# Two transformer layers on one core: the first two heads' score operands loaded ahead of the rest, and fewer unread products in front of them

## The reference, cut to what matters

```python
x = x + L0_attn(layernorm(x))      # rotary positions, 16 heads
x = x + L0_ffn(layernorm(x))       # one shared and 7 routed experts
x = x + L1_attn(layernorm(x))      # 16 heads
x = x + L1_ffn(layernorm(x))       # relative attention, then 32 experts
scores = q @ k.T / sqrt(8); out = softmax(scores) @ v
```

## Time and profile before

| what | value |
|---|---|
| median of three executions | 2069.04 us |
| the three | 2067.9, 2069.04, 2098.41 us |
| the profiled execution's own time | 2086.47 us |
| its span, first to last instruction | 2084.7 us |
| its mean granted clock of TensorE | 0.953 |
| PE busy / DVE busy / ACT busy | 94% / 66% / 58% of the span |

### The profile page before, as it was taken

The page is one execution under the profiler, slowest core; times in us unless marked ns, Lnnn a source line. Parts: engine busy times, 40 slices in busy tenths (PEclk is TensorE's granted clock), DMA queues, the critical chain, the costliest instruction groups (busy, mean ns, idle before and its releaser), DMA issues.

```text
span 2084.7 us, 40739 instructions
## 1 busy us (share of the span) xinstructions
PE 1966.8 (94%) x13972; PEld 1183.6 (57%) x13972; DVE 1379.4 (66%) x1770; ACT 1207.1 (58%) x2289; POOL 517.9 (25%) x501
## 2 busy tenths in 40 slices
PE   7999999799988999999769999999999999987998
PEld 4333334577764333333446666666666666665887
DVE  5999996656656689999554555545555455336776
ACT  2799999366641679999514444444444444443554
POOL 4000000278862000000032222222222222103654
PEclk9999999799997579999989999999999999988999
DMA  5333333131106123332341111221111122014654
GB/s 179 123 98 107 98 106 99 45 133 62 51 0 196 55 75 107 98 106 91 109 127 48 48 47 47 61 53 49 47 47 47 47 63 51 10 32 164 224 211 146
DMA packets 82559, 182.99 MB, mean 88 GB/s; under 512 B 16048, under 2 KB 45488, under 8 KB 77136
## 3 DMA queue, kind: packets, MB, share of 16 engines
q1 hardware_dynamic: 82448, 181.49, 28.0%
HBM read 146.83 MB, written 36.31 MB: 88 GB/s over the span
## 4 chain that ended last, share of the span: by engine, by line
PE 46%; DVE 2%; DMA 1%; SPq 1%; issue 0%; ACT 0%; DVEq 0%
PE PS L799 17%; PE PS L883 8%; PE PS L811 6%; PE PS L785 6%; PE PS L794 4%; PE PS L774 4%; DVE M L1278 1%; DMA Ks<-in_kv 0%; SPq L384 0%; PE PS L818 0%; PE PS L598 0%; PE PS L589 0%; PE PS L757 0%; DMA k_stack<-PR_r 0%; SPq L364 0%
## 5 line engine op out<-in xcount | busy, mean ns | idle before, releaser
L1257 DVE TENSOR_REDUCE M<-PS 128x1 f32<-128x1024 f32 x512 | 598.4, 1218 | 49.8 <-PE PS L676 44.9
L1540 ACT ACTIVATE PR<-PS 128x512 f32<-128x512 f32 x1024 | 540.1, 601 | 63.2 <-PE PS L691 42.7
L1577 ACT ACTIVATE PR<-PS 128x512 f32<-128x512 f32 x512 | 306.2, 599 | 376.9 <-PE PS L799 373.1
L1278 DVE TENSOR_REDUCE M<-PS 128x1 f32<-128x1024 f32 x256 | 311.9, 1222 | 219.3 <-PE PS L785 212.2
L701 PE MATMUL PS<-PR,Va 128*32 128x256 f32 x4096 | 343.6, 409 | 16.0 <-POOL Va L1724 7.7
L691 PE MATMUL PS<-Qs_r,Ks_r 25*128 25x512 f32 x1024 | 311.9, 520 | 0.0
L676 PE MATMUL PS<-Ks_r,Qs_r 24*128 24x512 f32 x1024 | 272.5, 527 | 1.7 <-DMA Ks_r<-k_stack 1.4
L676 PEld LDWEIGHTS PS<-Ks_r,Qs_r 24*128 24x128 f32 x1024 | 100.1, 192 | 217.8 <-issue 160.9
L1273 DVE TENSOR_TENSOR rt<-PS,rel 128x512 f32<-128x512 f32 x128 | 88.5, 691 | 159.4 <-PE PS L757 157.9
L701 PEld LDWEIGHTS PS<-PR,Va 128*32 128x32 f32 x4096 | 84.5, 110 | 154.3 <-issue 77.1
L1724 POOL TENSOR_TENSOR Va<-Vt,nil 128x64 f32<-128x64 f32 x96 | 28.0, 295 | 563.0 <-PE PS L701 559.5
(11 more groups left out here) (204 smaller groups left out, 3129.6 us busy)
## 6 DMA issues: line engine op xcount, KB each, us to landing
Qs<-g_dram SPq DMA_DIRECT2D x29, 1024.0 KB, 4.8
Ks_r<-k_stack SPq DMA_DIRECT2D x256, 100.0 KB
Qs_r<-q_stack SPq DMA_DIRECT2D x256, 96.0 KB
Qs_r<-q_stack SPq DMA_DIRECT2D x128, 128.0 KB
Ks_r<-k_stack SPq DMA_DIRECT2D x128, 128.0 KB
o_dram<-Ob SPq DMA_DIRECT2D x96, 128.0 KB, 2.7
Ks<-g_dram SPq DMA_DIRECT2D x10, 1024.0 KB, 4.9
q_stack<-BIG_r SPq DMA_DIRECT2D x18, 256.0 KB, 3.2
```

The source lines that it names most:

```text
L1257: e.tensor_reduce(M[:, s, qt:qt + 1], PS[:, 2 + 2 * (qt % 2):4 + 2 * (qt % 2), :] .rearrange("p a b -> p (a b)"), AX.X, ALU.max, negate=Tr ...
L1278: e.tensor_reduce(M[:, s, qt:qt + 1], PS[:, bk:bk + 2, :].rearrange("p a b -> p (a b)"), AX.X, ALU.max, negate=True).then_inc(max_done, 1)
L1540: e.activation(PR[:, kt % 4, qh * GW:(qh + 1) * GW], bank(RING[(x + turn) % 3]), ACT.Exp, scale=SCALE).then_inc(exp_done, 1)
L1577: e.activation(PR[:, kt % 4, qh * GW:(qh + 1) * GW], bank(TURN[kt % 2][qh]), ACT.Exp)\
```

## The change

It splits a head's eight loads into two halves, each with its own semaphore: row groups 2 and 3 count on the new `qm_in`, row groups 0 and 1 on `qk_in`, 64 each. Everywhere the halves are loaded in that order, groups 2 and 3 first. At the end of front(0) and front(2) only groups 2 and 3 of heads 0 and 1 are loaded at g == 2; the stores of g = 2 follow, and at g == 3 groups 0 and 1 of both heads come ahead of head 2. PE's scores wait for `qm_in`, and in `position` the waits for `qk_in` and `m_in` stand behind the first score pair. The unread products ahead of the first scores go from 26 to 16 (attention 0) and from 28 to 22 (attention 1).

```diff
+            def load_groups(n, s, groups, done, q_depth=MROW, k_depth=MROW + 1):
+                for to, of, depth in ((Qs_r, q_stack, q_depth), (Ks_r, k_stack, k_depth)):
+                    for r in groups:
+                        e.dma_start(to[r * KR:r * KR + depth, s, :].bitcast(F32),
+                                    of[bass.ds(n, 1), 0:depth, :].rearrange("n r t -> (n r) t")).then_inc(done[s], 16)
+
             def load_qk(n, s, q_depth=MROW, k_depth=MROW + 1):
-                for to, of, depth in ((Qs_r, q_stack, q_depth), (Ks_r, k_stack, k_depth)):
...
+                load_groups(n, s, (2, 3), qm_in, q_depth, k_depth)
+                load_groups(n, s, (0, 1), qk_in, q_depth, k_depth)
...
                             e.wait_ge(one_in, 16)
-                            load_qk(0, 0)
-                            load_qk(1, 1)
+                            load_groups(0, 0, (2, 3), qm_in)
+                            load_groups(1, 1, (2, 3), qm_in)
                     if g == 3 and f < 3:
+                        load_groups(0, 0, (0, 1), qk_in)
+                        load_groups(1, 1, (0, 1), qk_in)
                         load_qk(2, 2)
...
                     s2 = (s + 2) % SLOTS
-                    e.wait_ge(m_in[s], 32 * (NH // SLOTS * a + block + 1))
                     for kt in range(QT):
                         if ahead:
                             if kt == 0:
-                                e.wait_ge(qk_in[s2], 128 * (NH // SLOTS * a + block + (s >= 2) + 1))
+                                e.wait_ge(qm_in[s2], 64 * (NH // SLOTS * a + block + (s >= 2) + 1))
                             scores(n + 2, s2, kt)
+                        if kt == 0:
+                            e.wait_ge(qk_in[s], 64 * (NH // SLOTS * a + block + 1))
+                            e.wait_ge(m_in[s], 32 * (NH // SLOTS * a + block + 1))
                         turned(n, s, 2 * kt, turn)
...
-                keep_warm([26, 28][a], cols_=P)
+                keep_warm([16, 22][a], cols_=P)
                 products_read(4 * (a + 1))
                 for n in range(2):
-                    e.wait_ge(qk_in[n], 128 * (NH // SLOTS * a + 1))
+                    e.wait_ge(qm_in[n], 64 * (NH // SLOTS * a + 1))
...
                     if p == 0:
-                        e.wait_ge(qk_in[s], 128 * (2 * NH // SLOTS + block + 1))
+                        e.wait_ge(qm_in[s], 64 * (2 * NH // SLOTS + block + 1))
+                        e.wait_ge(qk_in[s], 64 * (2 * NH // SLOTS + block + 1))
```

More of the change, by code:

```diff
@@ L247, in two_layers @@
         qk_in = [sem(f"qk_in{s}") for s in range(SLOTS)]
+        qm_in = [sem(f"qm_in{s}") for s in range(SLOTS)]
         m_in = [sem(f"m_in{s}") for s in range(SLOTS)]
@@ L379, in attention_in @@
                     e.dma_start(atu[:, half, q], heads[:, g, 0:DH, :]).then_inc(at_in[half], 16)
+            def load_groups(n, s, groups, done, q_depth=MROW, k_depth=MROW + 1):
[3 more added lines that the diff above has]
+                                    of[bass.ds(n, 1), 0:depth, :].rearrange("n r t -> (n r) t")).then_inc(done[s], 16)
             def load_qk(n, s, q_depth=MROW, k_depth=MROW + 1):
-                for to, of, depth in ((Qs_r, q_stack, q_depth), (Ks_r, k_stack, k_depth)):
-                    for r in range(4):
-                        e.dma_start(to[r * KR:r * KR + depth, s, :].bitcast(F32),
-                                    of[bass.ds(n, 1), 0:depth, :].rearrange("n r t -> (n r) t")).then_inc(qk_in[s], 16)
+                load_groups(n, s, (2, 3), qm_in, q_depth, k_depth)
+                load_groups(n, s, (0, 1), qk_in, q_depth, k_depth)
             def load_rel(n, s):
```

## The result

| what | before | after |
|---|---|---|
| median, lowest to highest, 22 executions each | 2081.86, 2060.95 to 2107.93 us | 2086.22, 2070.13 to 2111.7 us |
| ratio of after to before, 95% interval | | 1.0055, 1.003 to 1.0081 |
| the profiled execution: time, span, mean clock | 2086.47, 2084.7, 0.953 | 2077.17, 2075.4, 0.963 |

The ratio leaves out the executions more than 1.5% above the fastest of their kernel (three of after's; the same mark takes nine of before's), and by it the change cost 0.55%; over all 22 the median is 0.21% above before's and the mean 0.18%, which executions that spread over more than 40 us do not tell from no change. Either way the 24.7 us that were forecast are not there, and the median of after lies above the predicted range of 2036 to 2076; so does the median that before has here.

What follows compares the result with a forecast made beforehand. DVE's row maxima bound the steady loop, PE only at low clock, so the first score's start and the clock count. Gains 2.1 + 2.7 + 37.3 = 42.1 from 2086.47 give 2044.4 us; range 2036 to 2076.

Steps and rivals of the forecast that it cites:

- First scores: First attention: first score at about 42.0 instead of 44.12, 2.1 us gained; second: 648.4 instead of 651.13, 2.7 us gained.
- my far end of 0.7: Before the first attention's first score: head 0's first half lands at 42.7 at latest, PE waiting 0.7 us; middle 41, no wait.
- The keys' hole: Before the second attention's first score: PE's 1.35 us standstill for head 0's keys goes, with the middle landing of 647.5.
- What is late next: Head 0's maxima row on SP lands by 59.5, wanted at 59.7; second attention 665.7, wanted at 666.2: margins 0.2 and 0.5.
- If they are missed, a few tenths: Before the first turned products: missing the maxima row's margins of 0.2 and 0.5 us costs only a few tenths.
- The clock: Second attention: the 1.35 us hole tipped the clock to 0.50; without it all 37.27 us go; bounds nothing to all.
- The rule set against the change: Ahead of the scores: activity releases the clock, so taking away 16 unread products removes what holds it; time as third rival.
- The third rival: First attention loses its clock too, between 16th product and first score, keys landing after 43.3: 37.3 us, 2083.8; chance 0.10.
- The stores: Third group's store, moved ahead of half the loads on SP, is reached at about 38.2, data ready 38.30: nothing to 0.1.
- the second halves: Second halves of heads 0 and 1, issued some 4 us later, land by 52 at latest, wanted at 59.7.
- The added waits: One more wait per head on PE, 48 in all: taken as zero, upper bound 1.4 us at 29 ns each.
- rivals 1 and 2: 1: clock falls all the same, 2064.2, chance 0.23. 2: head 0's half comes no earlier in second attention, about 2067, 0.11.

## Why the prediction was wrong, step by step

*First scores, right in the second attention, not in the first.* In the second, first load to first score took 9.87 us before and 7.14 after: 2.73 gained of 2.7 forecast. In the first nothing was gained in the profiled execution, 44.47 against 44.12. The front ran 3.25 us late (first load 38.58, 35.33), and the products began 0.97 us behind the first load instead of 2.89. The keys landed 4.46 us after their issue ended (40.01 to 44.47), close to the middle I took, but the products had ended at 43.29, and PE waited 1.18 us for `Ks_r<-k_stack`, beyond my far end of 0.7. Where that wait was absent, in the run with both rows on ACT's queue, the first score stood at 42.04, where 42.0 was forecast.

*The keys' hole, right in the second attention.* It went, with 22 products and no wait.

*What is late next, wrong; this is the step that failed.* I had the row "issued by 56.7, landed by 59.5 (2.8)" with margins of 0.2 and 0.5. Counted from the first score its issue ended no later than forecast (13.73 and 14.45 us; 14.7 and 14.5 forecast). But it landed 7.83 and 8.01 us after the issue instead of 2.8. I took the median time of the 32 KB loads of the relative attention for a row behind 36 other issues of the same queue in another stage. Nearer rows lay in the same stretch of the trace. The DMA issues of after, for 36 to 70 us, show the stores at 4.0 and 4.5:

```profile
q_stack<-BIG_r SPq DMA_DIRECT2D x6, 256.0 KB, 4.0
k_stack<-BIG_r SPq DMA_DIRECT2D x6, 256.0 KB, 4.5
```

Before had 3.9 and 4.6 there; with either the margin is negative, and its own row shows no more than a landing within 4.43. The divided loads let the scores start before the queue's other work was through, while the row stayed where it was in the queue. The bound of the kernel's start went from the keys to the row, and the step that counted on the margin had two tenths of it. The prediction had named a wait before the first turned product as a sign of being wrong, and none of its rivals rested on it.

*"If they are missed, a few tenths", wrong, and worse.* I priced the miss as its wait alone, though I had just argued that 1.35 us of hole cost 37.27. A price of that kind belonged to this hole too. Measured, hole and clock together: 10.85 and 16.60.

*The clock, right in part.* That a hole tips it was an inference from one pair. With the same wait and 22 products in it there was no fall, and all twelve waits for a maxima row in the profiles, 0.58 to 6.21 us, had a low stretch close behind. But the hole is not the whole cause. The keys' waits of 1.18 us in after's first attention and 0.59 in the first attention of before with 30 products were followed by none; with twelve products in the wait the clock fell behind 0.34 us, and with both rows on ACT's queue once behind no hole. The filled wait adds products and removes idle time in one, so it does not tell which of the two holds the clock. The loss is no constant: 4.5 to 37 us an attention, with the length of the low stretch. What tips the clock stays open.

*The rule set against the change.* The Trainium skill, "TensorE: Matmul & The Clock Gate", section "Part 1: The HAM clock gate", has the low clock as the default and activity as what releases it. The two runs with rows on ACT's queue and more unread products lean its way, in that none of their 24 executions lay above 2070; with the lower counts 13 of 16 stayed below 2058 all the same.

*The third rival* had the right sign and the wrong place: before the first score, where only 1.18 us of wait stood, instead of behind it. Its price of 37.3 was more than twice what either attention lost in the profiled execution. That its 2083.8 came near the measured 2086.22 is luck.

*The stores, the second halves:* no wait for either in the trace. *The added waits:* clean attentions of 317.90 and 317.93 beside 317.59 and 317.60 with before's waits, some 0.3 us each, in kernels that differ in the order of the loads too; I took zero with 1.4 as bound. The count was wrong: with 32 heads in each of three attentions the diff adds 96 waits, not 48, and the bound by the same 29 ns is 2.8.

*Not forecast:* from the second attention's last values to the end 5.23 us more. Before's loads have it too, with rows on ACT's queue (1085.25) and with 30 and 38 products (1088.14), so it is not the divided loads. Its cause stays open.

*The median.* The forecast started from the profiled execution, but rivals 1 and 2 and the upper end of the range from 2069.04, the median of three; twenty-two executions have 2081.86, with which rival 1 alone would stand at 2077.1, above the range. That before loses clock in every execution, for different lengths, fits its two profiles and stays an inference for the rest.

## What to carry to other kernels

When a start is pulled forward, list every transfer that the work behind it waits for, and take each landing from a row of the same queue in the same stretch, with what is queued ahead of it; a margin of some tenths on a landing is no margin. Price a missed margin at all that a standstill of PE has been seen to cost there, the clock included. A small transfer that is due soon belongs on a queue that is empty; where it can't come earlier, enough unread products to fill the wait can cost less than the wait left empty, as 22 did here and 12 did not.

## What the runs showed of the hardware

In the first attention with divided loads the row issued from ACT's queue was usable in 4.36 us or less, from SP's in 7.83, at the same place of the program and with a DMA share of 0.37 and 0.34 meanwhile. The Trainium skill, "DMA: Bandwidth & Descriptors", section "Issuing engines are not separate DMA queues", says that issuing from several engines saves only the issuing time. Here no issuing time was saved (53.65 on ACT, SP free at 53.47), and yet the row came 3.5 us or more sooner after its issue; where SP's transfers had run out early, in before, SP's row took no more than 4.43 either.

The low clock lasts far longer than the hole ahead of it: behind holes of 0.34 to 6.21 us PE ran at 0.50 for 17 to 102 us, busy almost without a break. The length differed from one execution of the same kernel to the next (102 and 57.7 us behind holes of 1.35 and 1.59). What ends it no run here shows.
